# Moving the last layer's output phase by phase, with the copy into time order and the store in the same step

## The reference

```python
def dense(x, emb, W0, b0, W1, b1, W2, b2, weight, bias_k):
    h = gelu(gelu(emb @ W0 + b0) @ W1 + b1)
    att = softmax(h @ W2 + b2)
    m = einsum('bk,koi->boi', att, weight[..., 0])
    return einsum('boi,bih->boh', m, x) + (att @ bias_k)[:, :, None]
def conv(x, c, weight, c_weight, bias):
    out = conv1d(x, weight, padding=4, groups=4)
    return out + (c @ c_weight.T)[:, :, None] + bias[None, :, None]
x = x + dense(x, ...L0); x = x + conv(x, ...L1)
x = x + dense(x, ...L2); x = x + conv(x, ...L3)
```

## Time and profile before

| what | value |
|---|---|
| time, median of 3 runs | 2628.59 us (2625.79 to 2630.22) |
| profiled execution, time | 2628.2 us |
| its span in the trace | 2626.3 us |
| PE busy | 2602.8 us, 99% |
| DVE busy | 2440.0 us, 93% |
| ACT busy | 2010.8 us, 77% |
| POOL busy | 791.5 us, 30% |
| DMA queue of SP, share of 16 engines | 58.6% |
| granted TensorE clock, mean | 0.997 |

### The profile page before, as it was taken

One profiled execution on the slowest core, in us unless ns is written; L12 is line 12 of the kernel. 1 busy time (PEld: TensorE's weight loads), 2 busy tenths in 40 slices (PEclk: granted clock), 3 DMA queues, 4 the chain that ended last, 5 costly groups with the idle time before them and its releaser, 6 DMA issues.

```text
span 2626.3 us, 107053 instructions
## 1 busy us (share of the span) xinstructions
PE 2602.8 (99%) x42610; PEld 1812.2 (69%) x42610; DVE 2440.0 (93%) x3218; ACT 2010.8 (77%) x3480; POOL 791.5 (30%) x1039
## 2 busy tenths in 40 slices
PE   8999999999999999999999999999999999999997
PEld 6667766776677667666766776677767766776765
DVE  7999999999999999999999999999999999999995
ACT  6777777777777777777777777777777777777774
POOL 0223222322332333223322332233223322322232
PEclk9999999999999999999999999999999999999999
DMA  4556655665666556555555665566556655655554
GB/s 147 182 183 195 194 182 185 194 192 182 187 192 194 182 187 196 189 182 187 195 190 182 190 199 183 182 194 196 181 182 193 197 181 182 196 194 182 184 185 159
DMA packets 228045, 489.80 MB, mean 187 GB/s; under 512 B 47016, under 2 KB 129072, under 8 KB 195376
## 3 DMA queue, kind: packets, MB, share of 16 engines
q1 hardware_dynamic: 228016, 489.39, 58.6%
HBM read 205.04 MB, written 150.99 MB: 136 GB/s over the span
## 4 chain that ended last, share of the span: by engine, by line
PE 96%; DVE 2%; SPq 1%; ACT 0%; issue 0%; DMA 0%; DVEq 0%; ACTq 0%
PE ps L376 41%; PE ps L355 28%; PE ps L327 14%; PE ps L342 13%; SPq L225 1%; DVE y L705 0%; DVE m_sum L657 0%; DMA m_parts<-mixed 0%; DVE prod L652 0%; ACT y_full L516 0%; PE ps L273 0%; SPq L215 0%; ACT y L516 0%; DVE y L699 0%; DVE xp L677 0%
## 5 line engine op out<-in xcount | busy, mean ns | idle before, releaser
L376 PE MATMUL ps<-y,conv_parts 32*128 32x512 f32 x18432 | 1129.5, 392 | 2.5 <-DVE y L705 1.2
L376 PEld LDWEIGHTS ps<-y,conv_parts 32*128 32x128 f32 x18432 | 925.5, 184 | 177.7 <-issue 46.9
L705 DVE TENSOR_TENSOR y<-y_full,y 128x512 fp32r<-128x512 f32 x1020 | 913.5, 956 | 115.3 <-ACT y L522 115.1
L516 ACT ACTIVATE y_full<-ps,bias 128x512 f32<-128x512 f32 x1018 | 654.0, 692 | 276.5 <-PE ps L327 170.6
L355 PE MATMUL ps<-y_full,conv_raw 32*32 32x512 f32 (+1 forms) x16384 | 754.1, 596 | 1.6 <-DVE y_full L738 1.6
L822 POOL COPY bias<-bias_table 128x4 f32 (+3 forms) x512 | 183.9, 373 | 1812.9 <-DMA o_ch<-o_ph 1660.0
L828 POOL COPY o_t<-o_ch 128x512 f32<-128x512 f32 x508 | 633.3, 1364 | 13.6 <-DMA o_ch<-o_ph 13.6
L522 ACT CAST y<-y_full 128x512 fp32r<-128x512 f32 x1020 | 559.0, 633 | 0.4 <-DVE y_full L738 0.4
L355 PEld LDWEIGHTS ps<-y_full,conv_raw 32*32 32x32 f32 (+1 forms) x16384 | 274.9, 117 | 409.3 <-issue 407.1
L571 ACT ACTIVATE o_ph<-ps,bias 128x512 f32<-128x512 f32 x381 | 234.3, 687 | 227.0 <-PE ps L376 227.0
L327 PEld LDWEIGHTS ps<-xp,m_own 128*128 128x128 f32 x1524 | 277.7, 189 | 163.0 <-issue 57.3
(11 more groups left out here) (61 smaller groups left out, 130.2 us busy)
## 6 DMA issues: line engine op xcount, KB each, us to landing
x_t<-x SPq DMA_DIRECT2D x128, 1024.0 KB, 5.4
o_ch<-o_ph SPq DMA_DIRECT2D x2032, 64.0 KB, 2.0
out<-o_t SPq DMA_DIRECT2D x127, 1024.0 KB, 4.1
m_parts<-mixed SPq DMA_DIRECT2D x512, 128.0 KB, 2.6
mixed<-m_own SPq DMA_DIRECT2D x128, 128.0 KB, 1.7
conv_raw<-conv_w SPq DMA_DIRECT2D x2, 768.0 KB, 9.8
mix_sb<-mix_w SPq DMA_DIRECT2D x2, 576.0 KB, 7.4
out<-x_t SPq DMA_DIRECT2D x4, 256.0 KB, 4.2
```

What stands on the lines that cost most here:

```text
L376: ins = nc.tensor.matmul(ps[:, bank + t, :], conv_parts[layer][rows, w, s - DENSE[0], :], src[rows, a, p_in, q:q + N], start=first, stop=f ...
L516: nc.scalar.activation(dst, src, ACT.Identity, bias=bias[layer][:, k % WIDTH[layer]:k % WIDTH[layer] + 1]).then_inc(done[layer], 1)
L705: nc.vector.tensor_tensor(dst, full, high.bitcast(fp32), ALU.subtract).then_inc(low_set[layer], 1)
```

## The change

SP now moves by phase: shuffle(j, p, first) waits for the whole result of sample j and for GpSimd's copy of phase p of the sample before, and issues the four groups of phase p. The 16 DMAs are the same 16. GpSimd waits for one phase, sets one bias, copies that phase, and goes on to the next phase, all in the step in which the moves are issued; SP stores the sample at the end of the same step. Before, the copies of a sample began after all 16 of its moves, in the step after. The biases of layers 1, 0, 2 and 3 are set in between; that of layer 2 is set for sample i+1 in step i and no longer for sample i.

```diff
-            def shuffle(j, g):
-                if g == G - 1:
-                    sp.wait_ge(phases_last, j + 1)
-                else:
-                    sp.wait_ge(phases_set, 3 * j + g + 1)
-                for p in range(PH):
+            def shuffle(j, p, first):
+                if p == 0:
+                    sp.wait_ge(phases_set, 3 * j + 3)
+                    sp.wait_ge(phases_last, j + 1)
+                if not first:
+                    sp.wait_ge(in_time_set, nth(j - 1, p))
+                for g in range(G):
                     sp.dma_start(o_ch[CG * g:CG * (g + 1), p, :], o_ph[CG * p:CG * (p + 1), g, :]).then_inc(shuffled[p], 16)
...
             def step(i, inner, odd):
-                if has(i, inner, 2):
-                    sp.wait_ge(in_time_set, 4 * (i - 1))
-                    sp.dma_start(out[i - 2], o_t[:]).then_inc(out_done, 16)
                 moves = has(i, inner, 1) and (inner or not is_last(i))
+                opening = not inner and i == 1
                 if moves:
-                    shuffle(i - 1, 0)
+                    shuffle(i - 1, 0, opening)
+                    shuffle(i - 1, 1, opening)
                 if has(i, inner, -1):
                     store_matrix(i + 1)
                 if moves:
-                    for g in range(1, G):
-                        shuffle(i - 1, g)
+                    shuffle(i - 1, 2, opening)
+                    shuffle(i - 1, 3, opening)
                 if has(i, inner, -1):
                     load_matrix(i + 1, False)
                 if has(i, inner, -3):
                     sp.wait_ge(x_low_set, 4 * (i + 2))
                     load_x(i + 3)
+                if moves:
+                    sp.wait_ge(in_time_set, 4 * i)
+                    sp.dma_start(out[i - 1], o_t[:]).then_inc(out_done, 16)
```

More of the change, by code:

```diff
@@ L822, in set_bias, with in_time, moved @@
                 nc.gpsimd.tensor_copy(bias[layer][:], bias_table[:, bass.ds(j, 1), COLUMN[layer]:COLUMN[layer] + WIDTH[layer]].rearrange("c j g -> c (j g)")).then_inc(bias_set[layer], 1)
-            def in_time(j):
+            def in_time(j, p):
                 ov = o_t[:].rearrange("c (n p) -> c p n", p=PH)
-                for p in range(PH):
-                    nc.gpsimd.tensor_copy(ov[:, p, :], o_ch[:, p, :]).then_inc(in_time_set, 1)
+                nc.gpsimd.tensor_copy(ov[:, p, :], o_ch[:, p, :]).then_inc(in_time_set, 1)
             def step(i, inner, odd):
[L831 to L840, removed]
+                moves = has(i, inner, 1) and (inner or not is_last(i))
+                def moved(p):
+                    if moves:
+                        pool.wait_ge(shuffled[p], 16 * G * i)
+                if moves and (inner or i > 1):
+                    pool.wait_ge(out_done, 16 * (i - 1))
+                moved(0)
                 if has(i, inner, -1):
@@ L843, in step @@
                     set_bias(1, i + 1)
+                if moves:
+                    in_time(i - 1, 0)
+                moved(1)
                 if has(i, inner, -2):
@@ L846, in step @@
                     set_bias(0, i + 2)
+                if moves:
+                    in_time(i - 1, 1)
+                moved(2)
+                if has(i, inner, -1):
+                    pool.wait_ge(full_set[2], 4 * (i + 1))
+                    set_bias(2, i + 1)
+                if moves:
+                    in_time(i - 1, 2)
+                moved(3)
                 if has(i, inner, 0) and (inner or i > 0):
@@ L850, in step @@
                     set_bias(3, i)
+                if moves:
+                    in_time(i - 1, 3)
             pool.wait_ge(first_in, 32)
```

## The result

The changed kernel takes 2659.49 us (median of 4 runs, 2658.56 to 2660.31) against 2627.19 for the kernel before on the same chip: a ratio of 1.0125, 95% interval 1.0113 to 1.0138. It is slower by 32 us. The forecast was 2642.2 with a range of 2624 to 2670: the sign and the place were right, the size is more than twice what I said (14.0 us above the profiled execution).

A forecast was written before the change was run, and what follows sets the result against it. PE, busy 99%, was taken as the bound, with DVE's chain to first_mix the closest. The profiled 2628.2 us plus 0.14 x 125 steps = 17.5 us of waits, minus 3.5 at the ends, gave 2642.2 us, range 2624 to 2670.

The forecast's parts named there:

- run of eight subtractions: DVE's low_2 and x_low, without a gap: copy 0 was to fall into low_2, copy 1 into x_low, both well inside.
- copy 2 beside low_1: On DVE: copy 2 comes at about 1321.6, after x_low, and does not hurt low_1, which has one input in PSUM.
- low_0's relief: On DVE: low_0, freed of the copies, takes 2.26 us less, which gains nothing on PE.
- Copy 3: On DVE: copy 3 may delay matrix(0) by up to 0.7 us; low_0 behind it still ends before dense(1) wants it.
- the chain grows by 2 x 0.74 = 1.48 us against a slack of 1.38: At first_mix on PE: two copies in low_2 and x_low exceed the slack, so PE waits 0.10 us every step.
- The price of a copy: On DVE: each copy that falls into a run of subtractions costs the run 1.42 - 0.68 = 0.74 us.
- The slack: From ACT's high_2 over low_2, x_low and low_1 to first_mix: 7.63 - 0.64 - 4.82 - 0.74 - 0.05 = 1.38 us.
- The 0.04 for starting anew: At first_mix: PE loses 0.04 us a step restarting behind a wait, read from 4.46 against 4.42 us for 72 matmuls.
- rival (a): At first_mix: the slack holds, the two copies cost 1.38 us or less; 2624.7, or up to 2633 us; chance 0.28.
- my 3.5: At the ends: 1.5 us from shorter matrix waits and 2.0 from last stores issued earlier, together -3.5 us.
- (b): In DVE's chain to first_mix: three collisions, or low_1 hurt; PE waits 0.88 us a step, 2735 us; chance 0.06.
- (c): On DVE: a copy blocks for its whole 1.12 us, by an exclusive port; 2737 us; chance 0.02.

The follow-up runs named there:

- e1: The changed kernel, with GpSimd setting biases 1 and 0 first, then waiting for x_low before copies 0 to 2, so none falls into the run: 2620.83 us, ratio 0.9976.
- e2: The changed kernel, with the bias of layer 0 and copy 1 waiting for x_low, so only copy 0 falls into the run: 2619.85 us, ratio 0.9972.
- e6: The changed kernel with all four copies writing densely, output left in phase order, both copies still in the run: 2619.61 us, ratio 0.9965.
- e8: The changed kernel, with the bias of layer 1 and copy 0 waiting for the end of low_2; only copy 0 hit the run, in x_low: 2618.91 us, ratio 0.9968.
- e5: The changed kernel plus a spare copy of phase 0 that writes every fourth element, ahead of its own copy: 2790.59 us, ratio 1.0605.
- e3: The changed kernel plus a spare, densely written copy of phase 0 ahead of its own copy, so three copies fall into the run: 2708.46 us, ratio 1.0308.
- e7: The kernel before with only SP's moves by phase; copies and store stay in the next step: 2623.47 us, ratio 0.9983.
- e4: The kernel before, moves still by group, with copies and store in the same step as the moves, behind all 16: 2628.22 us, ratio 1.0003.

## Why the prediction was right in place and wrong in size

**The place and the mechanism hold.** Two copies fall into the run of eight subtractions, copy 2 beside low_1 is free (2.71 us), first_mix waits, low_0's relief is worth nothing, and GpSimd, SP and the biases keep up. Copy 0 started 0.69 us behind low_2, copy 1 0.06 behind x_low, as reckoned within 0.1 us. Copy 3 did delay matrix(0), by 0.62 us, and PE did not notice. e1, e2 and e6 each take away one part of it, and with each the loss is gone.

**The step that failed is the sum "the chain grows by 2 x 0.74 = 1.48 us against a slack of 1.38".** Price and slack were off the same way, and a small third term had no ground:

- The price of a copy. 0.74 had been read at low_0. It is 0.76 in x_low and 0.85 in low_2, 1.61 together and 0.13 more than I said. e2 and e8 have the two prices with one copy alone. In e5, with copies close behind each other, the held-up instruction takes 1.46 to 1.55 us in low_2 and 1.40 to 1.49 in x_low, so the run that is held up sets most of the price, and what stands before a copy a few hundredths. Why low_2 pays more is open. Its output begins one element into the tile's row and x_low's does not; but so does low_0's, where the held-up rows of before are mostly 1.41 to 1.44. Nothing of this was tried.
- The slack. DVE follows ACT by 0.67 us at low_2, not by the 0.64 read at low_0; PE follows low_1 by 0.05 to 0.10, 0.08 on the mean, not by 0.05, a figure for which I had shown no row; and from high_2 to a first_mix that does not wait pass 7.60 us on the mean of e2, not the 7.63 of my one step. With these, 7.60 - 0.67 - 4.82 - 0.74 - 0.08 = 1.29 us. The steps give the threshold without these readings: against e2's 20.13 us (its run of 5.67 is free) the mean step after is 0.33 longer, with a run of 6.43, and that of e3 0.72 longer, with 6.84; 6.43 - 0.33 = 6.10, 6.84 - 0.72 = 6.12. In e5's step at 2010 the run is 7.22 and PE waits 1.04. 6.11 - 4.82 leaves 1.29 us again, 0.09 less than I had.
- The 0.04 for starting anew. There is no room for it in this sum, and its source was misread: no wait of PE is listed ahead of the row of 4.46 us, and the same 72 matmuls take 4.46 us in mid-loop too, right behind first_mix (at 2575.66 of before).

That makes 1.61 - 1.29 = 0.32 us a step by these terms, 0.33 measured, and not the 0.14 of the forecast. 0.14 x 125 had been 17.5 us; it is 41.5. Errors of 0.13 in 1.48 and 0.09 in 1.38 more than doubled the result, because it is their difference. I had named this in rival (a), but only as a way for the wait to vanish; the forecast's own range, 0.07 to 0.35 us a step, held it, the middle did not.

**Mid-loop and the end gave more than I took:** 3.8 us in mid-loop and 5.7 in the last stretch, 9.5 together for my 3.5. The second_mix of before, and the rows of after:

```profile
2600.55 4.62 PE L342 MATMUL ps<-y,m_parts 32*128 32x512 f32 x48 [2.86 <-DMA m_parts<-mixed]
...
2637.20 3.08 PE L345 MATMUL ps<-y,m_parts 32*128 32x512 f32 x48 [1.85 <-DMA m_parts<-mixed]
...
2650.84 0.37 SPq L256 DMA_DIRECT2D out<-o_t  x1
...
2653.77 2.15 SPq L260 DMA_DIRECT2D out<-x_t  x4
```

The wait for the matrix is 1.0 us shorter. The last second_mix takes 3.08 us where it took 4.62 before, 1.5 less, with the mean granted clock at 1.00 and not at 0.63 in these rows. I had not looked for that, and how far the shorter wait earned it is open (below). From the last regrouping on PE to the end of the span it is 6.9 us (2651.36 to 2658.3) and was 10.0 (2616.24 to 2626.3), 3.1 less: the four last stores are issued in 2.15 us and not in 3.83, and the first is not held up. e7 and e4 say which part does it: the moves by phase alone gain 5.6 us by the medians, 3.8 in mid-loop and 0.6 in the last stretch of the trace, but leave the last stores behind the store in front of them (e7); the same-step store alone gains nothing (e4); only together do they pull the last stores free. 41.5 - 3.8 - 5.7 = 32.0 us is the difference of the spans; the sum closes by the way it is made, since 41.5 and 3.8 are both counted against e2's steps. What supports the 41.5 by itself is the 0.32 us a step from prices and slack.

**Rivals.** (a) did not come: PE waits in all steps of the loop but one. (b) and (c), with 0.88 us a step and more, did not come either; that a copy blocks for its whole length is refuted by 0.76 to 0.85 against 1.12. The Trainium skill ("SBUF — State Buffer", section "Who interferes with whom") also says that a VectorE instruction with at most one SBUF input, outside the two-port modes, does not contend with GpSimd. For low_1, which has one input in PSUM, the traces agree: 2.71 to 2.73 us with a copy beside it.

## What to carry to other kernels

An engine at 93% behind a bound at 99% has a place in the step where its slack is largest; background work that shares something with it belongs there, and a change of order that moves it is a change of the critical chain, even if it touches neither engine. Where the answer is a small difference of two read numbers, read each at the very instruction that it will hit, and widen the forecast by their errors times the number of steps. And one wait placed so that background work starts behind the tight chain (e8, e1, e2) can be worth more than starting it as early as the data allow.

## What the runs showed that I had not expected

- A GpSimd copy of 128x512 that writes every fourth element takes 1.12 us alone and holds a two-input subtraction up by 0.74 to 0.85; the same copy written densely takes 0.61 (e6) and holds it up by 0.42. Either way it is some 0.2 to 0.4 us less than the copy's length.
- A tiny bias copy beside a subtraction takes longer (0.66 us and not 0.19, at 907.21 and 908.82 of before), but the subtraction keeps its 0.68.
- A wait of PE can be paid twice, but not every wait is. Behind 2.86 us (before), 2.41 (e7), 3.63 (e4) and also 1.80 (e3) of waiting, the last second_mix took 4.61 to 4.62 us; behind 1.85 (after), 1.71 (e1), 1.61 (e6), 1.60 (e5), 1.52 (e2) and 1.38 (e8) it took 3.08. At the start of the kernel, behind the same wait of 1.99 us, first_mix took 4.58 us in the profiled runs of before and after and 3.03 in that of e2, and in e5 waits of 1.83 to 1.89 us had both outcomes. The mean granted clock over the long rows is 0.63 (before, e3, e4, e7), over the short ones 1.00 (after, e2). So between 1.8 and 2.0 us the length of the wait does not decide it, and what does is open:

```profile
2683.39 4.61 PE L346 MATMUL ps<-y,m_parts 32*128 32x512 f32 x48 [1.80 <-DMA m_parts<-mixed]
```

- The fastest kernels with the whole work, e8 at 0.9968 and e2 at 0.9972, are below both the kernel before and e7 (0.9983) by medians, though their intervals overlap that of e7 (e6, at 0.9965, leaves the reorder out).
